# An attention and mixture-of-experts layer on one core: normalised input recomputed from kept moments, output bias by a product with ones, routing by maximum and minimum, counts by one scan

## The chip, the cores and the metric

The kernel runs on one core of a Trainium2 chip, written in Bass with semaphores placed by hand. The metric is the device time of one launch in microseconds (us). The engines are named as the profile names them: PE (TensorE; PEld is its weight load), DVE (VectorE), ACT (ScalarE), POOL (GpSimd), SP (SyncE, whose queue SPq issues nearly all DMAs).

## The reference, cut to what matters

```python
xn = _layernorm(x)                          # x: (2, 2048, 256) float32, no weights
x = x + _L0_attn_ref(xn, ...) + _L0_ffn_ref(xn, ...)

# inside _L0_ffn_ref(hidden_states = xn, ...), T = 4096 tokens, E = 16, D = 256, F = 1024
resid = hidden_states
x = layer_norm(hidden_states, ln1_w, ln1_b)
...                                          # q, k, v, causal attention, 16 heads of 16
hidden = resid + (ctx @ o_w + o_b)
resid = hidden
xt = layer_norm(hidden, ln2_w, ln2_b).reshape(T, D)
logits = xt @ router_w
probs = softmax(logits)
top1 = argmax(probs);  m1 = one_hot(top1, E)
top2 = argmax(where(m1 > 0, -inf, logits));  m2 = one_hot(top2, E)
loc1 = cumsum(m1, axis=0) - 1.0
loc2 = cumsum(m2, axis=0) - 1.0 + m1.sum(axis=0, keepdims=True)
m1 = m1 * (loc1 < C);  m2 = m2 * (loc2 < C)   # C = 512 places per expert
...                                          # gates, slots, 16 experts, combine
return resid + moe_out
```

Two attentions are computed, one with low-rank projections and one inside the feed-forward reference. Both read the normalised input `xn`, which is also the residual of the second part.

## The kernel before, in words

`layer` runs five stages one after the other, each an own block with a barrier between. Tokens are handled in 8 chunks of 512 (`NCH`, `CH`), a chunk being 4 tiles of 128 tokens (`TPC`).

**Stage A** (`stage_a`) loads x chunk by chunk, normalises it (`first_norm`, into `xn`), normalises that again for the second attention (`second_norm`, into `hn`), and makes q, k and v of both attentions in 17 PSUM units per chunk. q and k are split in two parts each (ACT writes the high part, DVE the low one) and stored in DRAM. SP issues, per chunk: the store of `xn` to the scratch tensor `xn_dram` (line 138), the load of x for the chunk after next (line 140), 16 stores of q and k parts (line 149), 2 stores of v (line 154). After chunk 5 it also issues the 14 loads of the first attention group (`load_piece`, lines 69 and 74). They stand in one queue.

**Stage B** (`stage_b`) is the two attentions, 16 groups of heads in an order written out by hand. The change leaves it as it is.

**Stage C** (`stage_c`) makes `hidden`, the second layer norm `xt` and the router's logits. For chunk c, PE computes `front(c)`: two PSUM banks of ctx @ o_w, 8 matmuls, which the trace records as 16 instructions. POOL computes `bias(c)`: o_b added in place to the chunk of `xn` loaded from DRAM (line 824). DVE computes `moments(c)`: bank + biased `xn` into `hidden` (line 862), then the statistics. ACT takes the root (line 901). DVE computes `norm(c)`: subtract and scale (line 882), times ln2_w (885), plus ln2_b (886), giving `xt_now`. PE then computes `back(c)`: 8 transposes (948), a wait for ACT's copies of them, and the logits (951). POOL also adds x to `hidden` into `base` (837), and once multiplies the last attention group by its reciprocals (841), behind the chunk 1 sum. Each engine has its own order: PE does front(0), front(1), and then for each c front(c+2) and back(c); DVE does moments(0), and then for each c moments(c+1) and norm(c); ACT root(c+1), back(c). Three places hold the loaded chunks, and SP loads chunk c+3 once the sum of chunk c is done.

**Stage D** (`stage_d`) routes. DVE works through one chain: softmax of the logits, `choose(0)`, `choose(1)`, `find_slots(0)`, `find_slots(1)`, the gates, and 8 rounds of `spread_tokens`, each of which builds one-hot matrices of 8 tiles. Nearly every step waits for the one ahead (`settle`). PE's order is fixed: 4 units of the output projection (`unit`, lines 1032 and 1034), `counts(0)`, 2 units, `counts(1)`, 10 units, and only then `collect`, which multiplies the one-hot matrices. `counts(n)` (lines 1040, 1041) sums the masks of choice n over the partitions and is what `find_slots(n)` waits for. `spread_tokens` has 4 places for its results (`RING`), so round 4 waits until `collect` has used round 0.

**Stage E** (`stage_e`) runs the 16 experts.

Of the kernel before, what the change touches and what calls it, by code (L numbers as in the profile page):

```python
# [76 lines left out]
def stage_a(nc, x, scratch, const, keep):  # L77

    xn_dram, q_dram, k_dram, v_dram = scratch
# [8 lines left out]
    with ExitStack() as ctx:  # L88
# [30 lines left out]
        xn_stored = [sem(f"xn_stored{i}") for i in range(2)]  # L119
# [5 lines left out]
        xn_chunks = xn_dram.rearrange("(c j p) d -> c p j d", j=TPC, p=P)  # L125
# [6 lines left out]
        def _(sp):  # L132
            for n in range(2):
                sp.dma_start(xs[:, n], x_chunks[n]).then_inc(x_in[n], 16)
            for c in range(NCH):
                u, b, cc = c % 2, c // (NCH // B), c % (NCH // B)
                sp.wait_ge(xn_ready, c + 1)
                sp.dma_start(xn_chunks[c], xn[:, u]).then_inc(xn_stored[u], 16)
# [22 lines left out]
            for n in range(2):  # L161
                sp.wait_ge(xn_stored[n], 16 * (NCH // 2))
                sp.wait_ge(v_stored[n], 16 * NCH)
# [4 lines left out]
        def _(dve):  # L168
# [5 lines left out]
            def norm(c, n, src, dst):  # L174
# [12 lines left out]
                dve.wait_ge(norm_step, done + 2)  # L187
                for j in range(TPC):
# [4 lines left out]
            def first_norm(i, u):  # L193
# [4 lines left out]
                dve.wait_ge(xn_stored[par], i * 16 + 16 * (u // 2))  # L198
                norm(c, 0, xs[:, par], xn[:, par]).then_inc(xn_ready, 1)
# [533 lines left out]
def stage_c(nc, x, scratch, const, keep):  # L733

    xn_dram, ctx_dram, xt_dram, rec_dram = scratch
# [4 lines left out]
    with ExitStack() as ctx:  # L740
# [7 lines left out]
        xn = sb("c_xn", [P, PLACES, TPC, D])  # L748
# [16 lines left out]
        biased = sem("biased")  # L765
# [17 lines left out]
        xn_chunks = xn_dram.rearrange("(c j p) d -> c p j d", j=TPC, p=P)  # L783
        xt_chunks = xt_dram.rearrange("(c j p) d -> c p j d", j=TPC, p=P)
        ARRIVED = 16 * 3

        @block.sync
        def _(sp):
            def load(c):
# [3 lines left out]
                sp.dma_start(xn[:, n], xn_chunks[c]).then_inc(arrived[n], 16)  # L793
# [27 lines left out]
        def _(pool):  # L821
            def bias(c):
                pool.wait_ge(arrived[c % PLACES], ARRIVED * (c // PLACES + 1))
# [5 lines left out]
            bias(0)  # L829
            for c in range(NCH):  # L830
                if c + 1 < NCH:
                    bias(c + 1)
# [11 lines left out]
        def _(dve):  # L844
# [8 lines left out]
            def moments(c):  # L853

                u = c % 2
                dve.wait_ge(biased, c + 1)
# [45 lines left out]

# [698 lines left out]
```

## Time and profile before

| what | value |
|---|---|
| median of 3 runs | 2394.43 us (2391.33 to 2430.84) |
| profiled execution | 2401.85 us, of which the span of the trace is 2400.1 us |
| mean granted PE clock | 0.95 of full speed |
| PE busy | 2243.1 us, 93% of the span |
| DVE busy | 1901.0 us, 79% |
| ACT busy | 1513.8 us, 63% |
| POOL busy | 495.8 us, 21% |

The shares are averages over five stages. Stage B alone takes from 227.9 to 1819.5 us, so that a share of the whole says little of the stages around it, which is where the change lies. Stages A, C and D have to be read in their own stretches of the trace. The 1.75 us by which the profiled execution is longer than its span lie outside the trace.

### The profile page before, as it was taken

The numbers are of one execution on the slowest core, as the hardware profiler recorded it, in microseconds if no ns is written. First come the engines' busy times: TensorE is split into PE (matmuls) and PEld (weight loads), VectorE is DVE, ScalarE is ACT, GpSimd is POOL, SyncE is SP. The second block draws the span as 40 slices with busy tenths as digits, with TensorE's granted clock in tenths as the row PEclk, the third lists the DMA queues.
The fourth block names the chain that finished last, engine by engine and source line by source line (L and its number), as shares of the span: only waits on it lengthen the run. The fifth ranks groups of instructions, "written<-read, shape, count | busy, mean of one in ns | idle before, by whom it ended". The sixth has DMA issues, their size and how long they took to land. (4 is left out here: it accounts for less than half of the span.)

```text
span 2400.1 us, 45293 instructions
## 1 busy us (share of the span) xinstructions
PE 2243.1 (93%) x15977; PEld 1289.1 (54%) x15977; DVE 1901.0 (79%) x5771; ACT 1513.8 (63%) x3190; POOL 495.8 (21%) x405
## 2 busy tenths in 40 slices
PE   5995999999999999999999999999996796999997
PEld 2553444444444444444444444444434675999997
DVE  3552999989999999898898998998944796666664
ACT  2541388778788787787777877877782212545443
POOL 0001000120211201202001011010004304777765
PEclk9997699999999999999999998999997798999999
DMA  5998325254154352441524516335115454445541
GB/s 154 292 267 226 36 29 64 36 66 57 27 73 51 41 64 39 63 57 27 73 36 57 64 23 78 42 42 69 16 20 155 148 172 115 109 111 120 125 118 31
DMA packets 145060, 203.62 MB, mean 85 GB/s; under 512 B 61066, under 2 KB 107872, under 8 KB 136544
## 3 DMA queue, kind: packets, MB, share of 16 engines
q1 hardware_dynamic: 132576, 191.08, 40.6%
q0 software_dynamic: 12288, 10.05, 3.3%
q8 instruction: 108, 1.77, 0.3%
q14 instruction: 88, 0.72, 0.1%
HBM read 134.24 MB, written 71.83 MB: 86 GB/s over the span
## 5 line engine op out<-in xcount | busy, mean ns | idle before, releaser
L652 ACT ACTIVATE probs<-s_banks 128x512 f32<-128x512 f32 (+3 forms) x2560 | 1182.4, 538 | 326.3 <-PE s_banks L603 198.3
L689 DVE TENSOR_REDUCE rowmax<-m_banks 128x1 f32<-128x512 f32 x1536 | 966.2, 682 | 66.8 <-PE m_banks L614 61.4
L614 PE MATMUL m_banks<-ks,qs 48*128 48x512 f32 (+3 forms) x2560 | 827.5, 436 | 28.6 <-PEq L88 20.5
L603 PE MATMUL s_banks<-qs,ks 50*128 50x512 f32 (+3 forms) x2560 | 819.7, 429 | 15.3 <-ACT probs L652 8.1
L632 PE MATMUL v_bank<-probs,vs 128*32 128x512 f32 (+3 forms) x5120 | 619.2, 556 | 0.0
L603 PEld LDWEIGHTS s_banks<-qs,ks 50*128 50x128 f32 x2560 | 401.5, 188 | 397.6 <-ACT probs L652 359.9
L614 PEld LDWEIGHTS m_banks<-ks,qs 48*128 48x128 f32 x2560 | 415.5, 193 | 262.0 <-DVE rowmax L689 162.9
L686 DVE CUSTOM_DVE_ANT_0 unused<-m_banks,c_maskq 128x128 bf16<-128x128 f32 (+3 forms) x1024 | 466.8, 486 | 59.9 <-issue 51.8
L549 POOL CAST nparts<-negmax 128x16 fp32r<-128x16 f32 x64 | 12.6, 197 | 1190.1 <-DVE negmax L695 1190.1
L1436 PE MATMUL e_banks<-w_parts,hid_parts 128*128 128x256 f32 x1536 | 189.7, 284 | 2.2 <-DVE hid_parts L1355 2.2
L575 PE MATMUL s_banks<-c_identb,c_later_col 64*128 64x64 bf16 x1024 | 188.8, 196 | 0.0
L575 PE MATMUL s_banks<-c_identb,c_later_col_swapped 64*128 64x64 bf16 x1024 | 188.5, 196 | 0.0
L1436 PEld LDWEIGHTS e_banks<-w_parts,hid_parts 128*128 128x128 f32 x1536 | 185.6, 192 | 3.8 <-DVE hid_parts L1355 2.5
L632 PEld LDWEIGHTS v_bank<-probs,vs 128*32 128x32 f32 x5120 | 101.5, 108 | 157.5 <-issue 80.4
L1421 PE MATMUL e_banks<-xinT,w_parts 128*128 128x512 f32 x768 | 179.4, 393 | 1.5 <-DVE xinT L1340 1.5
L1389 ACT ACTIVATE hid_parts<-e_banks,c_b1T 128x512 fp32r<-128x512 f32 x128 | 89.7, 701 | 114.7 <-PE e_banks L1421 102.8
L1421 PEld LDWEIGHTS e_banks<-xinT,w_parts 128*128 128x128 f32 x768 | 144.7, 190 | 31.5 <-issue 1.9
L1355 DVE TENSOR_TENSOR hid_parts<-e_hid,hid_parts 128x512 fp32r<-128x512 f32 x128 | 97.3, 776 | 47.3 <-ACT e_hid L1390 47.3
L1308 POOL DMA_INDIRECT out<-scaled,sums_of x64 | 113.1, 1767 | 36.9 <-POOL scaled L1302 23.3
L575 PEld LDWEIGHTS s_banks<-c_identb,c_later_col 64*128 64x128 bf16 x1024 | 95.4, 96 | 26.7 <-issue 6.2
L575 PEld LDWEIGHTS s_banks<-c_identb,c_later_col_swapped 64*128 64x128 bf16 x1024 | 94.8, 96 | 24.3 <-issue 12.1
L1302 POOL TENSOR_SCALAR scaled<-eout,slot_gates 128x256 f32<-128x256 f32 x64 | 95.9, 1545 | 54.5 <-DVE eout L1365 54.5
(185 smaller groups left out, 1744.1 us busy)
## 6 DMA issues: line engine op xcount, KB each, us to landing
w<-in_L_ffn_fc_w SPq DMA_DIRECT2D x32, 1024.0 KB, 4.9
qs<-q_scratch SPq DMA_DIRECT2D x96, 256.0 KB, 8.3
ks<-k_scratch SPq DMA_DIRECT2D x96, 256.0 KB, 10.0
q_scratch<-parts SPq DMA_DIRECT2D x64, 256.0 KB, 4.4
k_scratch<-parts SPq DMA_DIRECT2D x64, 256.0 KB, 4.5
v_scratch<-vt SPq DMA_DIRECT2D x16, 512.0 KB, 7.7
v_in<-v_scratch SPq DMA_DIRECT2D x32, 256.0 KB, 10.9
qs<-mrows SPq DMA_DIRECT2D x512, 2.0 KB
```

What stands on the lines that cost most here:

```text
L575: ins = pe.matmul(bank[:, j * HALF:(j + 1) * HALF], const[mask][rows, :], const["identb"][rows, rows], start=False, stop=j == 1)
L603: ins = pe.matmul(bank, ks[rows, slot, h // 2, k * P:(k + 1) * P], qs[rows, slot, h // 2, q * CH + first:(q + 1) * CH], start=True, stop=n ...
L614: pe.matmul(room(("M", NM * group + n))[:, 0:width], qs[rows, slot, h // 2, t * P:(t + 1) * P], ks[rows, slot, h // 2, c * CH:c * CH + wid ...
L632: ins = pe.matmul(v_bank[rows, first:CH], vs[:, slot, k, rows], probs[:, (n * GH + h) % PR, 0:CH - first], start=k == 0, stop=k == TPC * ( ...
L652: act.activation(probs[:, n % PR, 0:width], s_banks[:, (NS * group + n) % SRING, 0:width], ACT.Exp, scale=SCALE).then_inc(p_ready, 1)
L686: dve.tensor_tensor_reduce(unused[:, h, 0:width], scores, const["maskq"][:, CH - width:CH], 1.0, NEG, ALU.add, ALU.max, out).then_inc(m_us ...
L689: dve.tensor_reduce(out, scores, AX.X, ALU.max).then_inc(m_used, 1)
L1302: pool.tensor_scalar(scaled[:, u, j, :], eout[:, u, j, :], slot_gates[:, TPE * e + j:TPE * e + j + 1], None, ALU.mult).then_inc(weighed, 1)
L1308: pool.indirect_dma_start(out=rows, out_offset=bass.IndirectOffsetOnAxis(ap=sums_of[:, TPE * e + j:TPE * e + j + 1], axis=0), in_=scaled[: ...
L1355: dve.tensor_tensor(hid_parts[:, LO, f, :], hid[:, f % HRING, :], f32(hid_parts[:, HI, f, :]), ALU.subtract).then_inc(hid_split, 1)
L1421: last = pe.matmul(banks[:, HBANK + f % HRING, :], w1_parts[:, a, h, f * P:(f + 1) * P], xinT[:, b, h, :], start=h == 0 and (a, b) == PASS ...
L1436: last = pe.matmul(banks[:, OBANK + n, j * D:(j + 1) * D], hid_parts[:, a, f, tile * P:(tile + 1) * P], w2_parts[:, b, f, :], start=f == 0 ...
```

## The change

In stage A, `first_norm` keeps the reciprocal deviation and the negated mean of every token (`first_rstd`, `first_minus`, two small DVE instructions per chunk), and `xn` is no longer stored. In stage C nothing loads it. ACT makes `centred` = x - mean (`centre(c)`, 4 instructions per chunk), DVE multiplies by the kept reciprocal and adds the PSUM bank in one instruction per tile, and o_b enters the bank by one more matmul per tile: a row of ones times the row of o_b. POOL's bias step is gone. In stage D the two choices are found by a maximum, a comparison and a minimum over the expert's numbers, the totals are counted in expert order, and one scan over 512 columns with a zero at each expert's start replaces 16 scans over 32; several pairs of DVE instructions are joined to one.

```diff
@@ stage_a
-                sp.dma_start(xn_chunks[c], xn[:, u]).then_inc(xn_stored[u], 16)
...
+                if tiles is not None:
+                    dve.tensor_copy(const["first_rstd"][:, tiles], rstd[:, :])
+                    dve.tensor_scalar(const["first_minus"][:, tiles], meanvar[:, :, 0], -1.0, None, ALU.mult)
@@ stage_c, SP
-        ARRIVED = 16 * 3
+        ARRIVED = 16 * 2
-                sp.dma_start(xn[:, n], xn_chunks[c]).then_inc(arrived[n], 16)
@@ stage_c, POOL
-                pool.tensor_tensor(xn[:, c % PLACES], xn[:, c % PLACES],
-                                   const["ob"][:, :].unsqueeze(1).to_broadcast([P, TPC, D]), ALU.add).then_inc(biased, 1)
@@ stage_c, DVE
                 for half in range(2):
-                    pair = slice(2 * half, 2 * half + 2)
                     dve.wait_ge(front_ready, c * FRONT + half + 1)
-                    dve.tensor_tensor(hidden[:, u, pair, :], banks[:, BACK + u * FRONT + half, :].rearrange("p (j d) -> p j d", d=D),
-                                      xn[:, c % PLACES, pair, :], ALU.add).then_inc(hidden_ready, 1)
+                    for j in range(2):
+                        tile = 2 * half + j
+                        last = dve.scalar_tensor_tensor(out=hidden[:, u, tile, :], in0=centred[:, c % PLACES, tile, :],
+                                                        scalar=const["first_rstd"][:, c * TPC + tile:c * TPC + tile + 1],
+                                                        in1=banks[:, BACK + u * FRONT + half, j * D:(j + 1) * D],
+                                                        op0=ALU.mult, op1=ALU.add)
+                    last.then_inc(hidden_ready, 1)
@@ stage_c, ACT
+            def centre(c):
+                act.wait_ge(arrived[c % PLACES], ARRIVED * (c // PLACES + 1))
+                for j in range(TPC):
+                    last = act.activation(centred[:, c % PLACES, j, :], xs[:, c % PLACES, j, :], ACT.Identity,
+                                          bias=const["first_minus"][:, c * TPC + j:c * TPC + j + 1])
+                last.then_inc(centred_ready, 1)
+            centre(0)
+            centre(1)
             root(0)
             for c in range(NCH):
                 if c + 1 < NCH:
                     root(c + 1)
+                if c + 2 < NCH:
+                    centre(c + 2)
                 back(c)
@@ stage_c, PE, front(c)
                         for h in range(KD):
                             last = pe.matmul(bank[:, j * D:(j + 1) * D], attT[:, c % PLACES, h, tile * P:(tile + 1) * P],
-                                             const["ow"][:, h, :], start=h == 0, stop=h == KD - 1)
+                                             const["ow"][:, h, :], start=h == 0, stop=False)
+                        last = pe.matmul(bank[:, j * D:(j + 1) * D], const["ones"][0:1, :], const["ob"][0:1, :], start=False, stop=True)
@@ stage_d, PE, counts(n)
-                pe.matmul(banks[:, COUNTS + 2 * n + 1, :], const["ones"][:, :], m, start=True, stop=True).then_inc(counted, 1)
+                by_expert = mask[n][:, :, :].rearrange("p t e -> p e t")
+                pe.matmul(banks[:, COUNTS + 2 * n + 1, :], const["ones"][:, :], by_expert, start=True, stop=True).then_inc(counted, 1)
@@ stage_d, DVE, choose(n)
-                for t in range(NTILE):
-                    ins = dve.max(top8[:, t, :], src[:, t, :])
-                settle(ins)
-                for t in range(NTILE):
-                    ins = dve.max_index(top8_id[:, t, :], top8[:, t, :], src[:, t, :])
-                settle(ins)
-                settle(dve.tensor_copy(expert[n][:, :], top8_id[:, :, 0]))
-                dve.tensor_tensor(mask[n][:, :, :], experts.rearrange("p (t e) -> p t e", e=E), wide(expert[n][:, :]),
-                                  ALU.is_equal).then_inc(masks_ready, 1)
+                settle(dve.tensor_reduce(one[:, :], src[:, :, :], AX.X, ALU.max))
+                settle(dve.tensor_tensor(work[:, :, :], src[:, :, :], wide(one[:, :]), ALU.is_equal))
+                settle(dve.scalar_tensor_tensor(out=work[:, :, :].rearrange("p t e -> p (t e)"),
+                                                in0=work[:, :, :].rearrange("p t e -> p (t e)"), scalar=-float(E), in1=experts,
+                                                op0=ALU.mult, op1=ALU.add))
+                settle(dve.tensor_reduce(expert[n][:, :], work[:, :, :], AX.X, ALU.min))
+                dve.tensor_tensor(mask[n][:, :, :], work[:, :, :], wide(expert[n][:, :]), ALU.is_equal).then_inc(masks_ready, 1)
@@ stage_d, DVE, find_slots(n)
-                settle(dve.tensor_copy(total[:, :, :], banks[:, COUNTS + 2 * n + 1, :].rearrange("p (t e) -> p t e", e=E)))
-                for e in range(E):
-                    ins = dve.tensor_tensor_scan(upto[n][:, :, e], ones_cube[:, :], total[:, :, e], 0.0, ALU.mult, ALU.add)
-                settle(ins)
+                by_expert = banks[:, COUNTS + 2 * n + 1, :]
+                settle(dve.tensor_tensor_scan(upto[n][:, :], same_expert[:, :], by_expert, 0.0,
+                                              ALU.mult, ALU.add))
...
-                settle(dve.tensor_scalar(place[:, :, :], place[:, :, :], -1.0, None, ALU.add))
...
-                settle(dve.tensor_scalar(work[:, :, :], place[:, :, :], float(CAP), None, ALU.is_lt))
-                settle(dve.tensor_tensor(kept[n][:, :, :], work[:, :, :], mask[n][:, :, :], ALU.mult))
+                settle(dve.scalar_tensor_tensor(out=kept[n][:, :, :].rearrange("p t e -> p (t e)"),
+                                                in0=place[:, :, :].rearrange("p t e -> p (t e)"), scalar=float(CAP),
+                                                in1=mask[n][:, :, :].rearrange("p t e -> p (t e)"), op0=ALU.is_lt, op1=ALU.mult))
```

The part left out in `find_slots` joins the subtraction of one to the sum of places, and of the 11 instructions on 32 columns behind the slots makes 7.

On PE in stage C, this is what stands for front(2) and back(0) before; `c_ow` is o_w, `attT` the loaded context, `c_rw` the router's weights.

```order
L932 MATMUL c_banks<-c_ow,attT 128x256 [waits hidden_ready,arrived2]
L932 MATMUL c_banks<-c_ow,attT 128x256 x3
L932 MATMUL c_banks<-c_ow,attT 128x256 [waits hidden_ready]
L932 MATMUL c_banks<-c_ow,attT 128x256 x3
L948 MATMUL c_banks<-c_ident,xt_now 128x128 [waits c_xt_ready]
L948 MATMUL c_banks<-c_ident,xt_now 128x128 x7
```

And this is the same place in the changed kernel.

```order
L935 MATMUL c_banks<-c_ow,attT 128x256 [waits hidden_ready,arrived2]
L935 MATMUL c_banks<-c_ow,attT 128x256
L937 MATMUL c_banks<-c_ob,c_ones 128x256
L935 MATMUL c_banks<-c_ow,attT 128x256 x2
L937 MATMUL c_banks<-c_ob,c_ones 128x256
L935 MATMUL c_banks<-c_ow,attT 128x256 [waits hidden_ready]
L935 MATMUL c_banks<-c_ow,attT 128x256
L937 MATMUL c_banks<-c_ob,c_ones 128x256
L935 MATMUL c_banks<-c_ow,attT 128x256 x2
L937 MATMUL c_banks<-c_ob,c_ones 128x256
L952 MATMUL c_banks<-c_ident,xt_now 128x128 [waits c_xt_ready]
```

Four matmuls of 256 columns stand in front(c) that were not there; nothing else of PE's order moves.

On ACT in stage C the start before is this.

```order
L901 ACT_TABLE_LOAD
L901 ACTIVATE c_std<-c_meanvar,c_eps 128x4 [waits c_var_ready] x2
L912 ACTIVATE xtT<-c_banks 128x512 [waits back_ready] x2
L912 ACTIVATE logits<-c_banks 128x64 [waits back_ready]
L901 ACTIVATE c_std<-c_meanvar,c_eps 128x4 [waits c_var_ready]
```

In the changed kernel it is this.

```order
L898 ACTIVATE centred<-c_xs,c_first_minus 128x256 [waits arrived0]
L898 ACTIVATE centred<-c_xs,c_first_minus 128x256 x3
L898 ACTIVATE centred<-c_xs,c_first_minus 128x256 [waits arrived1]
L898 ACTIVATE centred<-c_xs,c_first_minus 128x256 x3
L893 ACT_TABLE_LOAD
L893 ACTIVATE c_std<-c_meanvar,c_eps 128x4 [waits c_var_ready] x2
L898 ACTIVATE centred<-c_xs,c_first_minus 128x256 [waits arrived2]
L898 ACTIVATE centred<-c_xs,c_first_minus 128x256 x3
L911 ACTIVATE xtT<-c_banks 128x512 [waits back_ready] x2
```

The table load moved behind two chunks of `centred`, and a wait for chunk c+2's loads now stands ahead of back(c)'s copies.

## Rows read from the trace of the kernel before

**Rows 1.** Busy time by stretch: us, PE, PEld, DVE, ACT, POOL, PEclk, DMA share, GB/s
```profile
1819.50:1918.00 98.50, 69.61 (x320) 59.39 (x320) 70.03 (x145) 13.79 (x33) 46.95 (x23) 0.74 0.61 182
...
147.00:168.00 21.00, 19.03 (x68) 11.34 (x67) 11.09 (x36) 10.73 (x19) 0.00 (x0) 1.00 0.96 301
205.00:210.00 5.00, 2.55 (x12) 1.90 (x10) 2.48 (x4) 1.87 (x4) 0.00 (x0) 1.00 1.04 388
```

**Rows 2.** Timeline of SP in stage A: start, us, instruction, times
```profile
181.82 11.34 SPq L138 DMA_DIRECT2D xn_scratch<-xn  x1
...
205.75 1.20 SPq L138 DMA_DIRECT2D xn_scratch<-xn  x1
```

**Rows 3.** Timeline of PE in stage C, in brackets the idle time ahead
```profile
1826.93 13.89 PE L932 MATMUL c_banks<-c_ow,attT 128*128 128x256 f32 x48 [8.31 <-DMA c_xs<-in_L_attn_x]
1850.16 1.97 PE L948 MATMUL c_banks<-c_ident,xt_now 128*128 128x128 f32 x8 [9.34 <-DVE xt_now L886]
...
1856.25 5.62 PE L932 MATMUL c_banks<-c_ow,attT 128*128 128x256 f32 x16
1861.71 1.04 PE L948 MATMUL c_banks<-c_ident,xt_now 128*128 128x128 f32 x8
...
1865.29 3.70 PE L932 MATMUL c_banks<-c_ow,attT 128*128 128x256 f32 x16
...
1891.67 6.67 PE L932 MATMUL c_banks<-c_ow,attT 128*128 128x256 f32 x16
```

**Rows 4.** Timeline of DVE in stage C
```profile
1839.69 3.72 DVE L882 TENSOR_SCALAR xt_now<-hidden,c_meanvar,c_rstd 128x256 f32<-128x256 f32 x4
...
1844.70 5.40 DVE L886 TENSOR_TENSOR xt_now<-xt_now,c_ln2b 128x1024 f32<-128x1024 f32 x1
...
1861.91 0.69 DVE L862 TENSOR_TENSOR hidden<-c_banks,c_xn 128x512 f32<-128x512 f32 x1 [1.07 <-PE c_banks L932]
...
1864.56 1.60 DVE L882 TENSOR_SCALAR xt_now<-hidden,c_meanvar,c_rstd 128x256 f32<-128x256 f32 x4
...
1868.59 1.28 DVE L862 TENSOR_TENSOR hidden<-c_banks,c_xn 128x512 f32<-128x512 f32 x2
...
1879.99 5.08 DVE L882 TENSOR_SCALAR xt_now<-hidden,c_meanvar,c_rstd 128x256 f32<-128x256 f32 x4
```

**Rows 5.** Timeline of POOL in stage C
```profile
1843.45 5.57 POOL L841 TENSOR_TENSOR rden<-rden,pv_last 128x2048 f32<-128x2048 f32 x1 [0.84 <-DMA rden<-rec_scratch]
...
1879.57 2.35 POOL L824 TENSOR_TENSOR c_xn<-c_xn,c_ob 128x1024 f32<-128x1024 f32 x1 [6.38 <-DMA c_xs<-in_L_attn_x]
```

**Rows 6.** Timeline of DVE in stage D
```profile
1922.06 2.54 DVE L1132 MAX8 top<-d_probs 128x8 f32<-128x16 f32 x32
...
1939.32 0.69 DVE L1149 COPY d_total<-d_banks 128x512 f32<-128x512 f32 x1
1940.05 2.09 DVE L1151 TENSOR_TENSOR_SCAN upto<-ones_cube,d_total 128x32 f32<-128x32 f32 x16
...
1947.43 0.18 DVE L1165 TENSOR_SCALAR d_one<-slot 128x32 f32<-128x32 f32 x1
...
1949.85 0.69 DVE L1149 COPY d_total<-d_banks 128x512 f32<-128x512 f32 x1
...
1954.61 2.72 DVE L1159 TENSOR_TENSOR d_place<-d_place,upto 128x512 f32<-128x512 f32 x1
...
1969.36 0.69 DVE L1181 TENSOR_TENSOR in_cell<-numbers,cell 128x512 f32<-128x512 f32 x1
...
1996.11 0.22 DVE L1205 TENSOR_SCALAR d_row<-d_banks 128x64 f32<-128x64 f32 x1 [2.14 <-PE d_banks L1047]
```

**Rows 7.** Timeline of PE in stage D
```profile
1936.81 1.02 PE L1041 MATMUL d_banks<-mask,c_ones 128*128 128x512 f32 x2
...
1943.71 1.02 PE L1041 MATMUL d_banks<-mask,c_ones 128*128 128x512 f32 x2
...
1970.03 0.59 PE L1034 MATMUL d_banks<-base,c_ident 128*128 128x256 f32 x2
```

More of the change, by code:

```diff
@@ L77, in stage_a @@
 def stage_a(nc, x, scratch, const, keep):
-    xn_dram, q_dram, k_dram, v_dram = scratch
+    q_dram, k_dram, v_dram = scratch
     UNITS = 17
@@ L172, in _, with norm @@
             dve.memset(none[:, 3:4], 0.0).then_inc(unit_ready, 2 * UNITS)
-            def norm(c, n, src, dst):
+            def norm(c, n, src, dst, tiles=None):
                 done = c * 4 + 2 * n
@@ L197, in first_norm @@
                 dve.wait_ge(unit_ready, c * UNITS + C_UNIT)
-                dve.wait_ge(xn_stored[par], i * 16 + 16 * (u // 2))
-                norm(c, 0, xs[:, par], xn[:, par]).then_inc(xn_ready, 1)
+                norm(c, 0, xs[:, par], xn[:, par], bass.ds(i * (2 * TPC) + u * TPC, TPC)).then_inc(xn_ready, 1)
             def second_norm(i, u):
@@ L855, in moments @@
                 u = c % 2
[L856 removed]
+                dve.wait_ge(centred_ready, c + 1)
                 if c >= 2:
@@ L986, in stage_d @@
         kept = [sb(f"kept{n}", cube) for n in range(2)]
-        upto = [sb(f"upto{n}", cube) for n in range(2)]
-        place, total, work = sb("d_place", cube), sb("d_total", cube), sb("d_work", cube)
-        top8 = sb("top8", [P, NTILE, 8])
-        top8_id = sb("top8_id", [P, NTILE, 8], U32)
+        upto = [sb(f"upto{n}", [P, E * NTILE]) for n in range(2)]
+        place, work = sb("d_place", cube), sb("d_work", cube)
         expert = [sb(f"expert{n}", flat) for n in range(2)]
@@ L1148, in find_slots @@
                 dve.wait_ge(counted, n + 1)
-                settle(dve.tensor_copy(total[:, :, :], banks[:, COUNTS + 2 * n + 1, :].rearrange("p (t e) -> p t e", e=E)))
-                for e in range(E):
-                    ins = dve.tensor_tensor_scan(upto[n][:, :, e], ones_cube[:, :], total[:, :, e], 0.0, ALU.mult, ALU.add)
-                settle(ins)
-                settle(dve.tensor_tensor(work[:, :, :], upto[n][:, :, :], total[:, :, :], ALU.subtract))
-                settle(dve.tensor_tensor(place[:, :, :], banks[:, COUNTS + 2 * n, :].rearrange("p (t e) -> p t e", e=E),
-                                         work[:, :, :], ALU.add))
@@ L1157, in find_slots @@
+                settle(dve.scalar_tensor_tensor(out=place[:, :, :].rearrange("p t e -> p (t e)"), in0=banks[:, COUNTS + 2 * n, :],
+                                                scalar=-1.0, in1=work[:, :, :].rearrange("p t e -> p (t e)"),
+                                                op0=ALU.add, op1=ALU.add))
                 if n == 1:
-                    firsts = upto[0][:, NTILE - 1:NTILE, :].to_broadcast(cube)
+                    firsts = upto[0][:, :].rearrange("p (e t) -> p t e", e=E)[:, NTILE - 1:NTILE, :].to_broadcast(cube)
@@ L1166, in find_slots @@
                 for q in range(2, TPE):
-                    settle(dve.tensor_scalar(two[:, :], slot[n][:, :], float(q * P), None, ALU.is_ge))
-                    settle(dve.tensor_tensor(one[:, :], one[:, :], two[:, :], ALU.add))
-                settle(dve.tensor_scalar(two[:, :], one[:, :], -float(P), None, ALU.mult))
-                settle(dve.tensor_tensor(slot[n][:, :], slot[n][:, :], two[:, :], ALU.add))
-                settle(dve.tensor_scalar(two[:, :], any_kept[n][:, :], -float(CELLS), float(CELLS), ALU.mult, ALU.add))
-                settle(dve.tensor_tensor(one[:, :], one[:, :], two[:, :], ALU.add))
-                settle(dve.tensor_scalar(two[:, :], expert[n][:, :], float(TPE), None, ALU.mult))
+                    settle(dve.scalar_tensor_tensor(out=one[:, :], in0=slot[n][:, :], scalar=float(q * P), in1=one[:, :],
+                                                    op0=ALU.is_ge, op1=ALU.add))
+                settle(dve.scalar_tensor_tensor(out=slot[n][:, :], in0=one[:, :], scalar=-float(P), in1=slot[n][:, :],
+                                                op0=ALU.mult, op1=ALU.add))
+                settle(dve.scalar_tensor_tensor(out=one[:, :], in0=expert[n][:, :], scalar=float(TPE), in1=one[:, :],
+                                                op0=ALU.mult, op1=ALU.add))
+                settle(dve.tensor_scalar(two[:, :], any_kept[n][:, :], -float(CELLS), float(CELLS + E * TPE), ALU.mult, ALU.add))
                 settle(dve.tensor_tensor(cell[n][:, :], one[:, :], two[:, :], ALU.add))
@@ L1543, in layer @@
                   "ln1w": [P, KD], "ln1b": [P, KD], "qb": [P, KD], "kb": [P, KD], "ln2w": [P, D], "ln2b": [P, D],
-                  "b1T": [P, E * F // P], "ident": [P, P], "upper": [P, P], "ones": [P, P], "eps": [P, 1], "maskq": [P, CH]}
+                  "b1T": [P, E * F // P], "ident": [P, P], "upper": [P, P], "ones": [P, P], "eps": [P, 1], "first_rstd": [P, NTILE], "first_minus": [P, NTILE], "maskq": [P, CH]}
         const = {n: ctx.enter_context(nc.sbuf_tensor(f"c_{n}", s, F32)) for n, s in shapes.items()}
@@ L1572, in layer @@
                     nc.sbuf_tensor("numbers", [P, NUMBERS_SIZE], F32) as numbers:
-                stage_c(nc, x, (xn_dram, ctx_dram, xt_dram, rec_dram), const, ((base, logits, numbers), last))
+                stage_c(nc, x, (ctx_dram, xt_dram, rec_dram), const, ((base, logits, numbers), last))
                 stage_d(nc, (w["fc1_w"], w["fc2_w"]), (ctx_dram, xt_dram, out), const, (base, logits, numbers), keep)
```

25 lines of the change are left out of this document (9 added, 16 removed).

## The prediction

> **What bounds the kernel now.** I read the busy times by stretch first, then the timelines of the stretches that the change touches. The reader is to see that each has another bound, so that no share of the whole span prices an edit.
>
> Stage A: in a chunk's 21 us PE is busy 19.0 at full clock while the DMA engines are busy 0.96 [rows 1]. PE paces it and the DMA is just behind. Once the loads for the attention are queued as well, SP stands 11.34 us in the issue of one store of `xn` [rows 2], and at 205 to 210 us the DMA share is over 1 at 388 GB/s while PE is half idle [rows 1]. So the end of stage A is paced by DMA.
>
> Stage C: 98.5 us, PE busy 69.6, DVE 70.0, the granted clock 0.74 on the mean [rows 1]. Neither fills it. PE's undisturbed turn is a back of 1865.29 - 1861.71 = 3.58 us and a front of 3.70, less 0.16 by which instructions overlap: 7.1 us [rows 3]. DVE's is longer, because some of its instructions last several times their size: four of line 882 take 1.60 us at one place, 3.72 and 5.08 at others, and one of line 886 takes 5.40 us [rows 4]. At those places POOL runs: its multiply from 1843.45 for 5.57 us, its bias from 1879.57 [rows 5]. DVE waits for POOL there. These instructions read only SBUF. The Trainium skill ("SBUF — State Buffer", section "SBUF: two separate sides") says that DVE instructions with two SBUF inputs or in a two-port mode and GpSimd lock one port pair for a whole instruction; the rows agree.
>
> Stage D: DVE's chain runs from 1922.06 to 1996.11 [rows 6]; PE's units end at 1970.03 + 0.59 = 1970.6 [rows 7], and only behind them can the one-hot products start. DVE's first round starts at 1969.36 [rows 6], so the two arrive together. That decides the worth of a shorter routing.
>
> **Stage A, part by part.** Eight stores of 0.52 MB go. Six of them lie where PE paces: nothing is gained. Two, at 181.82 and 205.75 [rows 2], lie in the stretch that DMA paces: at 388 GB/s 1.35 us each, 2.7 us. The second blocked SP for 1.20 us, which agrees. If only the second counts it is 1.35; at the 301 GB/s of the paced chunk [rows 1] and with a third store's backlog carried in, 5.2. I keep 1 to 6 as ends. I take -3.0, near the saturated row. The 11.34 us of the first is a wait for room in the queue; the next store inherits it. Two instructions of 4 columns are added on DVE before each `xn`; beyond the first chunk DVE is half idle, and in the first they cost some 0.2 us.
>
> **Stage C, start.** The first chunk's loads shrink from three of 0.52 MB to two. They landed at 1826.93, 7.4 us behind the stage's start [rows 3]; a third of what is beyond 2 us of latency is 1.6 us, so PE starts at about 1825.3. But each front now has 24 instructions for 16. At full clock one is 3.70 / 16, less the overlap of the last, 0.216 us; at the lower level, half the clock, 0.43. The first bank needs 12 instructions for 8 while PE is at the lower level (1.7 us more), which eats the gain: hidden(0) is ready at the same time as now. Front(1) is 1.7 us longer, so moments(1) ends at 1841.6 instead of 1839.5. Norm(0) then meets POOL's long multiply, as now: its loads come earlier, but the sum of chunk 1 stands ahead of it on POOL and ends 1842.3, the multiply at 1847. DVE finishes norm(0) at about 1850.6; now 1844.70 + 5.40 = 1850.1 [rows 4]. So +0.5 there. ACT's `centre` is hidden: four instructions of 256 columns in the 8 us in which ACT waits, its table load too, and PE's product is later than both. The new wait for chunk c+2's loads ahead of back(c)'s copies is covered: those loads are issued two turns before.
>
> **Stage C, middle.** PE, idle since 1844, does back(0) at the lower level as now (6.1 us [rows 3]). Front(3) took 5.62 us, its clock rising at its end; with 24 instructions it ends at about 1864.0 instead of 1861.9, and hidden(3) comes 2.1 us later than now. From there PE's turn is 24 x 0.216 = 5.2 for the front and 3.58 for the back, 8.8 us. DVE's turn, freed of the bias: 1868.59 - 1864.56 = 4.03 for norm, 1864.56 - 1861.91 = 2.65 for half of hidden and the statistics, 0.6 for its other half (1.28 for both) [rows 4], and 0.1 to 0.3 because hidden is four instructions for two at the same columns (four of line 882 take 1.60, two of line 862 1.28): about 7.5. **PE takes over as the bound**, and what DVE is freed of is late nowhere. Four such turns behind front(3): 1864.0 + 4 x 8.8 = 1899.2 for front(7)'s end, where it now ends at 1891.67 + 6.67 = 1898.3 [rows 3], because DVE's turns and the clock hold it there. The tail, DVE's norm(6) and (7) and two backs, is the same. So stage C loses 0.8 us if PE stays at its full clock. But front(7) now runs mostly at the lower level, 3.0 us longer (6.67 for 3.70 [rows 3]); PE has smaller gaps in the change, so I take three quarters of one such front, 2.3. Stage C: **+3.1 us**. The nearest rows bound a K=1 matmul by the price of the full one above and by nothing below; at zero stage C would fall to DVE's turn, -6 to -7 us. The price by columns is the nearer: the records of equal columns are equal in the trace, whatever the tile. The Trainium skill ("TensorE: Matmul & The Clock Gate", section "Why this matters for your kernels") says that a single matmul with 32 rows takes as long as one with 128. No row here has a matmul of one row; by that page the sum stays as it is.
>
> **Stage D.** A choice is now (1939.32 - 1922.06 - 3 x 0.73) / 2 = 7.5 us without mask and second logits, an instruction of 512 columns being 0.73 with its wait (1940.05 - 1939.32 [rows 6]). The new one has four: 2.9. Both masks are ready at 1922.06 + 5 x 0.73 + 0.73 + 5 x 0.73 = 1930.0 instead of 1939.3. **But find_slots(0) waits for counts(0)**, whose place on PE is behind four units: it ends at 1936.81 + 1.02 = 1937.8 [rows 7]. Of 9.3 us saved 1.5 arrive. Find_slots(0) took 10.5 us (1949.85 - 1939.32). Now: a scan, six of 512 columns at 0.73, seven small at 0.22 (11 took 1949.85 - 1947.43). The scan over 512 columns lies between 0.69, a copy of as many, and 2.1, the sixteen; from 2.09 / 16 = 0.130 for 32 columns, at 1 column per cycle or 2 cycles per column, I take 1.15. Sum 7.1: to 1944.9. Counts(1) ends at 1944.7, just in time. Find_slots(1) has one more of 512: 7.8, to 1952.7. The gates took 4.2, and POOL's split of w1 (which held line 1159 for 2.72 instead of 0.69 and the next one too, 4.1 us) comes at the same time by ACT's clock and is met again, now by the gates: 1961.0. Four rounds of 3.07 ((1993.97 - 1969.36) / 8, the last ending 2.14 before 1996.11): 1973.3. Round 4 needs the first `collect`, behind the units: 1970.6 + 1.9 = 1972.5. So the rounds go on without a wait: last at 1985.5, its product 2.1 later, 1987.6 for 1996.11. **-8.5 us**; -9.3 is the most while PE's units stand, -8 with a slower scan, -6.5 if the strided reads of the counts double them. The Trainium skill ("DVE: opcode table, instruction layouts, handler registers and perf-mode slots", section 6) says that this scan runs at half throughput, which would be an estimated 1.13 us; the trace's 32-column scans fit it, and the sum would not move.
>
> **Sum.** -3.0 + 0.2 + 3.1 - 8.5 = -8.2 us on a span of 2400.1. The profiled execution, 2401.85, would be 2393.6; that execution lies 7.4 above the median, and the prediction is put on the median: 2394.4 - 8.2 = **2386 us**. A gain or loss of some 2% (48 us) is about what a measurement of this kernel can tell from no change.
>
> **Rivals.** (1) DVE still paces stage C, because a product with ones is cheap: DVE's 7.5 us turn for four chunks is 30.0 where the ends of front(3) and front(7) now lie 1898.3 - 1861.9 = 36.4 apart [rows 3]: -6.4 instead of +3.1, total -17.7, 2377. For it: only one row of the array is filled. Against: records go by columns. 0.17. (2) Slower: PE sits at its lower clock through stage C. There the mean is 0.74 already, and the idle time ahead of back(0) stays (6 to 7 us). At the lower level a turn of 8.8 is 16.5. Two more of the five turns that way (+15.4) give +7, 2402; all five +30, 2425. It decides against the change from about one turn on (8.2 / 7.7). 0.13. (3) The stage A relief is larger, since the DMA share of 0.96 is nearly a bound in each chunk: every store worth 1.35, 11 us: 2378. Against: PE is dense there. 0.06. (4) The routing is not held by PE's order and the whole 16 us arrive: 2378. Against: the orders are fixed in program. 0.04. My forecast: 0.60.
>
> **How the numbers follow.** The forecast's own bounds are -1 to -6 in A, -2 to +8 in C, -9.3 to -6.5 in D: 2377 to 2396. Rivals 1, 3 and 4 stretch the low end to 2374, rival 2 the high end to 2400, beyond which part of it stays. No case but the extreme of rival 2 nears 48 us: faster 0.01, within 0.97, slower 0.02.
>
> **What the profile would show.** Right: the time from stage C's start to its end 98 to 105 us, PE's front rows at x24 and about 5.3 us with no wait of line 882 over 2 us except by the multiply; DVE in stage D idle about 7 us ahead of the scan, released by the count's matmul; the one-hot rounds without gaps; stage A shorter by 3. Wrong: a front of 24 in under 4.5 us, PE's clock under 0.6 in stage C, DVE's wait ahead of the scan missing, or stage B or E changed by several us, which nothing here prices.

## The result and the profile after

The changed kernel took 2456.39 us (median of 4, 2447.35 to 2475.16) beside 2398.84 us for the kernel before: ratio 1.0228, 95% interval 1.0182 to 1.0275. It is slower, by 44 to 66 us, where 2386 was forecast; whether by more than 2% the interval leaves open. The profiled execution took 2475.16 us, its span 2473.4.

By stretch the place is plain. These are windows of the changed kernel: stage B, stage C, and the 81 us from stage D's start; the columns are those of [rows 1].

```profile
223.20:1841.60 1618.40, 1594.14 (x12352) 739.14 (x12352) 1413.23 (x4689) 1215.65 (x2689) 159.92 (x169) 0.94 0.37 46
...
1842.40:1999.27 156.87, 144.31 (x384) 93.51 (x384) 65.54 (x161) 27.30 (x65) 25.50 (x15) 0.51 0.30 88
1999.27:2080.27 81.00, 64.45 (x329) 54.61 (x330) 58.93 (x98) 13.36 (x20) 9.39 (x6) 0.90 0.46 137
```

Stage C lasts 156.9 us for 98.5 [rows 1], 58.4 more. DVE does less there than before (65.5 us for 70.0), PE is busy 144.3 us for 69.6, and its granted clock fell from 0.74 to 0.51 (of its two levels the lower is 0.50). Stage B takes 1618 us for 1592, which the change doesn't touch; in the twelve kernels below, which share stage B, it took 1588 to 1619 with no relation to the edit. That is scatter of single executions, not the change (the other three of this kernel had spans of 2445.6 to 2458.3).

PE's timeline in stage C shows why it is busy:

```profile
1848.08 2.07 PE L935 MATMUL c_banks<-c_ow,attT 128*128 128x256 f32 x4 [6.61 <-DMA c_xs<-in_L_attn_x]
...
1904.60 1.97 PE L952 MATMUL c_banks<-c_ident,xt_now 128*128 128x128 f32 x8
1907.26 3.59 PE L955 MATMUL c_banks<-c_rw,xtT 128*128 128x16 f32 x16 [0.69 <-ACT xtT L911]
1910.69 2.05 PE L935 MATMUL c_banks<-c_ow,attT 128*128 128x256 f32 x4
1912.67 1.22 PE L937 MATMUL c_banks<-c_ob,c_ones 1*128 1x256 f32 x2
1913.82 2.08 PE L935 MATMUL c_banks<-c_ow,attT 128*128 128x256 f32 x4
...
1923.28 1.97 PE L952 MATMUL c_banks<-c_ident,xt_now 128*128 128x128 f32 x8
```

PE waits for little more than ACT's copies, 0.69 us a turn (a turn is the time from one chunk's back to the next one's), and yet every instruction has its price at the lower level: eight transposes are 1.97 us, where they were 1.04 in an undisturbed turn [rows 3]. The turn is 1923.28 - 1904.60 = 18.68 us; all eight chunks go that way. From 1848.08 to the first back at 1885.92 PE runs three fronts without a wait, and the level doesn't change. Before, the same three took 13.89 us [rows 3], less than 48 x 0.43 = 20.6, so the clock came up within them. A tile takes 1913.82 - 1910.69 = 3.13 us, though six instructions of 256 columns at 0.43 are 2.6. The rest is seen in the weight loads:

```profile
1848.08 1.35 PEld L935 LDWEIGHTS c_banks<-c_ow,attT 128*128 128x128 f32 x4 [6.88 <-DMA c_xs<-in_L_attn_x]
1850.09 0.50 PEld L937 LDWEIGHTS c_banks<-c_ob,c_ones 1*128 1x128 f32 x2 [0.65 <-issue]
1851.23 1.35 PEld L935 LDWEIGHTS c_banks<-c_ow,attT 128*128 128x128 f32 x4 [0.65 <-issue]
```

At each change between 128 rows and one, the load stands still for 0.65 us before it starts: it isn't drawn ahead of the running matmul, as it is between instructions of equal rows. A tile has two such switches, and its 0.55 us beyond the columns make some 0.3 us of each. The 32 tiles of the stage have some 18 us of them, which the trace counts as busy time of PE. DVE now waits for PE at each half:

```profile
1898.50 0.87 DVE L851 SCALAR_TENSOR_TENSOR hidden<-centred,c_first_rstd,c_banks 128x256 f32<-128x256 f32 x2 [5.52 <-PE c_banks L937]
1904.71 0.87 DVE L851 SCALAR_TENSOR_TENSOR hidden<-centred,c_first_rstd,c_banks 128x256 f32<-128x256 f32 x2 [5.34 <-PE c_banks L937]
```

In stage D the DVE's chain came shorter as meant. Its rows, and PE's of the count ahead of it:

```profile
2019.88 1.22 DVE L1152 TENSOR_TENSOR_SCAN upto<-same_expert,d_banks 128x512 f32<-128x512 f32 x1 [8.03 <-PE d_banks L1044]
2021.13 1.03 DVE L1154 TENSOR_TENSOR d_work<-upto,d_banks 128x512 f32<-128x512 f32 x1
...
2027.98 1.22 DVE L1152 TENSOR_TENSOR_SCAN upto<-same_expert,d_banks 128x512 f32<-128x512 f32 x1 [0.64 <-PE d_banks L1044]
...
2070.15 0.23 DVE L1208 TENSOR_SCALAR d_row<-d_banks 128x64 f32<-128x64 f32 x1 [2.14 <-PE d_banks L1050]
```

```profile
2017.03 1.02 PE L1042 MATMUL d_banks<-mask,c_upper 128*128 128x512 f32 x2
2017.89 1.88 PE L1044 MATMUL d_banks<-mask,c_ones 128*128 128x512 f32 x2
```

From the stage's start to the last product's reading it is 2070.15 - 1999.27 = 70.9 us for 1996.11 - 1918.0 = 78.1 [rows 1, 6]: 7.2 less.

### The profile page after: what moved, and what is told of

The parts are those of the page before. It is cut to its first block and busy times, and to the rows that moved or that the text cites. A ratio compares the mean times of both kernels' runs of the same rounds, so it can differ in the third digit from the quotient of the medians.

```text
span 2473.4 us, 45239 instructions
## 1 busy us (share of the span) xinstructions
PE 2341.5 (95%) x16041; PEld 1325.7 (54%) x16041; DVE 1883.0 (76%) x5574; ACT 1526.5 (62%) x3222; POOL 473.1 (19%) x397
## 5 line engine op out<-in xcount | busy, mean ns | idle before, releaser
L630 PE MATMUL v_bank<-probs,vs 128*32 128x512 f32 (+3 forms) x5120 | 635.8, 570 | 0.0
```

The costliest lines, as they stand in the source:

```text
L630: ins = pe.matmul(v_bank[rows, first:CH], vs[:, slot, k, rows], probs[:, (n * GH + h) % PR, 0:CH - first], start=k == 0, stop=k == TPC * ( ...
```

## The experiments

The theory (A): a product with few rows takes PE's clock away in all of stage C, and nothing else in the change costs. The rivals: (B) any six instructions for four overload PE, whatever their rows; (C) the loss is in the recomputation (ACT's centring, the new waits, the loads). All runs stand in one table, then one by one. Stage C is counted from its first load's issue to stage D's, in one profiled execution. Where the last column says "one run", that execution is all there is, and no ratio is given. Two kernels leave something out of the result: "no product" all of o_b, "in one tile of four" o_b in three tiles of four.

| kernel | stage C, us | clock in it | ratio to before (95%) |
|---|---|---|---|
| before | 98.5 | 0.74 | |
| changed: 1 row | 156.9 | 0.51 | 1.0228 (1.0182 to 1.0275) |
| before with the 1-row product alone | 158.6 | 0.51 | 1.0221 (1.0148 to 1.0294) |
| 32 rows | 156.9 | 0.51 | 1.0193 (1.0113 to 1.0272) |
| 64 rows | 156.8 | 0.51 | one run |
| 96 rows | 107.3 | 0.75 | one run |
| 128 rows | 103.9 | 0.78 | 0.9997 (0.9954 to 1.0040) |
| 128 rows, 127 of them zero | 102.9 | 0.77 | 0.9996 (0.9955 to 1.0037) |
| 1 row, in one tile of four | 105.6 | 0.71 | one run |
| 1 row, two products together | 125.1 | 0.69 | one run |
| no product, no o_b | 83.5 | 0.80 | 0.9880 (0.9803 to 0.9958) |
| o_b by POOL again | 94.8 | 0.77 | 0.9981 (0.9939 to 1.0024) |
| 128 rows of bf16 | 91.9 | 0.77 | 0.9918 (0.9890 to 0.9946) |
| before with stage D's part alone | 101.5 | 0.75 | 0.9976 (0.9953 to 0.9998) |

**The product alone, put into the kernel before.**

```diff
@@ kernel before, stage_c: bias(c) of POOL removed, DVE waits for the loads
-                                             const["ow"][:, h, :], start=h == 0, stop=h == KD - 1)
+                                             const["ow"][:, h, :], start=h == 0, stop=False)
+                        last = pe.matmul(bank[:, j * D:(j + 1) * D], const["ones"][0:1, :], const["ob"][0:1, :], start=False, stop=True)
```

> The kernel before with only one part of the change: o_b by the one-row product, POOL's bias step gone, everything else as before; nothing is left out. Theory A: this part alone gives the whole loss: PE at its lower clock through stage C, turn 18 to 19 us, stage C about 158 us, the time 1.02 to 1.03 of before. Theory C: stage C no slower than 105 us.

It has the whole loss: 158.6 us, 1.0221. Theory C falls, since nothing is recomputed here.

**No product.** The product with ones is removed from the changed kernel.

> The changed kernel without the product with ones: o_b is left out of the result. Theory A and theory B both: PE's front is 16 instructions again and the clock as before, stage C paced by DVE at about 7.6 us a turn, 88 to 98 us in all, the time 0.987 to 0.995 of before. A third theory (C: ACT's centring or the shorter loads slow stage C): stage C stays over 120 us.

83.5 us. DVE's turn, freed of POOL's bias, is the pace: the rows of line 874 lie 1879.82 - 1872.18 = 7.64 apart.

```profile
1872.18 1.60 DVE L874 TENSOR_SCALAR xt_now<-hidden,c_meanvar,c_rstd 128x256 f32<-128x256 f32 x4
...
1879.82 1.59 DVE L874 TENSOR_SCALAR xt_now<-hidden,c_meanvar,c_rstd 128x256 f32<-128x256 f32 x4
```

**128 rows of ones** (o_b divided by 128, made once by DVE; `ob_part`).

```diff
-                        last = pe.matmul(bank[:, j * D:(j + 1) * D], const["ones"][0:1, :], const["ob"][0:1, :], start=False, stop=True)
+                        last = pe.matmul(bank[:, j * D:(j + 1) * D], const["ones"][0:128, :], ob_part[0:128, :], start=False, stop=True)
```

> The changed kernel with o_b brought in by a product of 128 rows of ones with 128 equal rows of o_b / 128, in place of one row of each; nothing is left out. Theory A (products with one row keep PE at its lower clock and make their neighbours' weight loads wait): PE reaches full clock in stage C, the turn falls from 18.7 to about 9 us, stage C from 158 to about 102 us, the time to 0.99 to 1.00 of before. Theory B (any extra product in the front does it, because the fronts and backs together are what keeps the clock low): stage C stays over 140 us and the time at 1.02 of before.

The count, the columns and the result are the same, and stage C is 53 us shorter. Theory B falls as the cause of the loss. By the rows above, some 18 us of the 53 are the switches, and the other 35 are the clock (an estimate from 32 tiles at 0.55 us). What B has right is smaller: the product of 128 rows still costs 103.9 us for 83.5 without one. PE's rows, all at full clock but for the front's start at 1879.81:

```profile
1876.09 1.04 PE L955 MATMUL c_banks<-c_ident,xt_now 128*128 128x128 f32 x8
...
1879.81 2.05 PE L938 MATMUL c_banks<-c_ow,attT 128*128 128x256 f32 x4
...
1886.61 1.04 PE L955 MATMUL c_banks<-c_ident,xt_now 128*128 128x128 f32 x8
1888.39 1.96 PE L958 MATMUL c_banks<-c_rw,xtT 128*128 128x16 f32 x16 [0.74 <-ACT xtT L914]
1890.19 1.11 PE L938 MATMUL c_banks<-c_ow,attT 128*128 128x256 f32 x4
1891.14 0.59 PE L940 MATMUL c_banks<-ob_part,c_ones 128*128 128x256 f32 x2
...
1895.46 1.04 PE L955 MATMUL c_banks<-c_ident,xt_now 128*128 128x128 f32 x8
```

The turn from 1886.61 is 8.85 us, a tile 0.95 + 0.43, without a switch's gap. The backs ahead of it start at 1855.02, 1865.56 and 1876.09, so the three turns before took 10.5 us each, with the first instructions of each front at the lower level: the clock falls for some microseconds in these even with full rows.

**32, 64 and 96 rows**, the same edit with another number.

> As the run with 128 rows, but 32 rows of ones times 32 rows of o_b / 32. Theory A, if what counts is the share of the rows filled: between one row and 128, PE at full clock for part of stage C, 105 to 140 us. If what counts is that the product spans fewer rows than the next one at all: as with one row, 150 us or more. Theory B: as with one row.

> The changed kernel with 64 rows in the product (ones times o_b / 64). One and 32 rows gave the same stage C of 157 to 158 us, 128 rows 104. If the loss grows as rows are left empty, 64 rows lie between, near 130 us. If it has an edge between 32 and 128 rows, 64 give one of the two, 104 or 157. If it comes from changing the rows between two instructions (the weight load is then not hidden), 64 rows give 157.

> The changed kernel with 96 rows in the product (ones times o_b / 96). One, 32 and 64 rows gave 157 us for stage C, all with the clock at 0.51; 128 rows 103 to 104. If only a full array counts, or if the switch between row counts does it, 96 rows give 157 too; if there is an edge in the number of rows below 96, they give 104.

32 and 64 rows are as slow as one, 96 nearly as fast as 128. There is an edge between 64 and 96. The first product of the stage, 64 rows and then 96:

```profile
1818.77 1.22 PE L940 MATMUL c_banks<-ob_part,c_ones 64*128 64x256 f32 x2
```

```profile
1826.84 1.06 PE L940 MATMUL c_banks<-ob_part,c_ones 96*128 96x256 f32 x2
```

Both are at the lower level, and the 64 rows last 0.16 longer; 128 rows take 1.06 there too. The weight loads of 96 rows have no idle time ahead of them at either level (the row shown is at full clock), those of 64 have 0.65 us as with one row:

```profile
1830.32 0.41 PEld L940 LDWEIGHTS c_banks<-ob_part,c_ones 96*128 96x128 f32 x2
```

```profile
1818.77 0.50 PEld L940 LDWEIGHTS c_banks<-ob_part,c_ones 64*128 64x128 f32 x2 [0.65 <-issue]
```

So the edge in the clock and the edge in the switch lie in the same interval of rows.

**Rows or data.** 128 rows are named, of which 127 hold zero.

```diff
+            settle(dve.memset(first_row[:, :], 0.0))
+            dve.memset(first_row[0:1, :], 1.0).then_inc(ob_ready, 1)
-                        last = pe.matmul(bank[:, j * D:(j + 1) * D], const["ones"][0:1, :], const["ob"][0:1, :], start=False, stop=True)
+                        last = pe.matmul(bank[:, j * D:(j + 1) * D], first_row[:, :], const["ob"][:, :], start=False, stop=True)
```

> The changed kernel with a left side of 128 rows in the product, of which only the first is not zero, and o_b's 128 equal rows as the right side: the sum is exactly o_b, as in the changed kernel, and only the rows that the instruction spans differ. If what counts is the rows that the instruction names, stage C comes out as with 128 rows of ones, 104 us and a ratio of 1.00. If what counts is data that are not zero, or only the work done, it comes out as with one row: a turn of 18.7 us, stage C 155 to 160 us, ratio 1.02.

Stage C took 102.9 us. The rows that the instruction names count, not what is in them.

**How many, and how divided.** First one product for four tiles (`if tile == 0`), then as many as in the changed kernel, two at a time:

```diff
+                for j in range(2):
+                    for k in range(FRONT):
+                        pe.matmul(fronts[k][:, j * D:(j + 1) * D], const["ones"][0:1, :], const["ob"][0:1, :], start=True, stop=False)
+                    for k in range(FRONT):
+                        tile = 2 * k + j
+                        for h in range(KD):
...
```

> The changed kernel with the one-row product in the first tile of each chunk alone; o_b is left out of the other three tiles. If each product costs what it lasts, a quarter of the loss against the kernel without products is left: (158 - 83.5) / 4, stage C 102 us. If a few such products are enough to hold the clock down, PE stays at 0.5 and a turn is 18.7 less three products of 0.61 and three switches of 0.3: 16.0 us, stage C 135 us. If it takes many to hold it down, the clock is up again in most of the stage and stage C is under 95 us.

> The changed kernel with the same one-row products, as many and as long, but two of them together (one for each bank) ahead of the tiles that they belong to, so that PE changes between 128 rows and one four times in a chunk instead of eight, and runs eight instructions of 128 rows in a row instead of four. If it is the share of time in products of few rows that holds the clock down, it stays at 0.51 and a turn is 18.7 less two pairs of switches, 4 x 0.3 = 1.2 at most: 17.5 us, stage C 147 to 152 us. If it is the switch, or how long PE runs full arrays without a break, the clock comes up in part or in whole: stage C 105 to 130 us. One product in four tiles, with sixteen in a row between, gave 105.6 with the clock up in the first chunk.

One in four gave 105.6 us, near what the first case of its expectation said (102), but not for its reason: the clock came up while one-row products went on, and sank again. The pairs gave 125.1, below what the share of time says (147 to 152). The clock changes inside the stage, at the same instructions. These are the rows of the pairs:

```profile
1845.21 2.07 PE L933 MATMUL c_banks<-c_ob,c_ones 1*128 1x256 f32 x4
1847.21 3.78 PE L937 MATMUL c_banks<-c_ow,attT 128*128 128x256 f32 x8
1850.92 1.13 PE L933 MATMUL c_banks<-c_ob,c_ones 1*128 1x256 f32 x4
1851.98 2.00 PE L937 MATMUL c_banks<-c_ow,attT 128*128 128x256 f32 x8
...
1903.77 2.07 PE L933 MATMUL c_banks<-c_ob,c_ones 1*128 1x256 f32 x4
```

So the share of time in few rows alone doesn't decide: as many of them, in fewer and longer pieces, let the clock up now and then, to 0.69 on the mean. At full clock the weight loads still wait at each change of rows, 0.33 us for 0.65.

**o_b by POOL, xn made by ACT** (scale and bias in one pass, the kept constant being the mean times the reciprocal deviation).

> The changed kernel without the product: stage A keeps the mean times the reciprocal deviation, ACT makes the whole normalised input in stage C, and POOL adds o_b to it as in the kernel before; stages A and D as changed. Stage A is 4.7 us shorter than before and stage D 7.0; stage C keeps the turns of the kernel before with its first loads 1.7 us earlier: 95 to 100 us. Sum -12 to -15 us, ratio 0.994 to 0.995. If the changed kernel's loss were in the recomputation and not in the product, stage C would stay at 150 us and the ratio over 1.015.

Stage C is 94.8, just under the expected 95 to 100; the ratio is 0.9981, with an interval that takes in both one and the expected 0.994. So the recomputation doesn't cause the loss. POOL's step costs here too: line 860 waits 2.25 us for it in two of the last four chunks.

**128 rows of bf16.** o_b as three bf16 parts in rows 0, 32 and 64, the others zero.

```diff
+            for i in range(3):
+                last = dve.tensor_copy(ob_rows[32 * i:32 * i + 1, :], ob_b[i][32 * i:32 * i + 1, :])
...
-                        last = pe.matmul(bank[:, j * D:(j + 1) * D], const["ones"][0:1, :], const["ob"][0:1, :], start=False, stop=True)
+                        last = pe.matmul(bank[:, j * D:(j + 1) * D], ones_b[:, :], ob_rows[:, :], start=False, stop=True)
```

> The changed kernel with o_b in three bf16 parts (their sum is o_b to 24 bits) in rows 0, 32 and 64 of a 128-row right side that is zero elsewhere, and a 128-row left side of bf16 ones. A float32 product of 256 columns is two instructions; in bf16 it is one. If what counts is the rows that an instruction spans, and the rest is plain columns, PE stays at full clock and a front costs 3.70 + 4 x 0.11 = 4.1 us, PE's turn 7.6 like DVE's 7.64: stage C 84 to 87 us, ratio 0.987 to 0.992, faster than both kernels. If bf16 or rows of zeros keep the clock down, stage C is at 130 or over. If the change of type costs a switch, at most 0.3 us twice a tile, a turn is 9 to 10 us and stage C 95 to 105 us.

It took 2385.36 us beside 2403.61: **0.9918, faster than the kernel before** by 0.5 to 1.1%, and by its ratio faster than the changed one. A product is one instruction, and the next matmul starts 0.11 us behind it (1838.59 - 1838.48):

```profile
1838.48 0.27 PE L952 MATMUL c_banks<-ob_rows,ones_b 128*128 128x256 bf16 x1
1838.59 1.03 PE L950 MATMUL c_banks<-c_ow,attT 128*128 128x256 f32 x4
...
1883.40 1.04 PE L967 MATMUL c_banks<-c_ident,xt_now 128*128 128x128 f32 x8
...
1890.97 1.04 PE L967 MATMUL c_banks<-c_ident,xt_now 128*128 128x128 f32 x8
```

PE's turn is 7.57 here and DVE's 7.64, so that neither waits for the other. Stage C was 91.9, not 84 to 87: POOL's multiply held line 882 for 5.40 us, and three of PE's turns took 11.8, 9.2 and 9.2, with part of each front at the lower level. One of them is the turn from the last row shown: the clock, once up, fell again.

**Stage D's part alone.**

> The kernel before with stage D of the changed kernel and nothing else. If stage D's gain is its own, DVE's chain there is 70.2 us for 78.0 and the time 7 to 8 us less: ratio 0.997. If the gain came from what stage C leaves (PE's clock, or loads issued at another time), the chain is 78 us as before. Stage C 98 to 99 us in both.

DVE's chain took 1990.70 - 1920.33 = 70.4 us for 78.1: the gain is its own. The 101.5 us of its stage C, whose code is that of before, show that one profile tells a stage to some 3 us.

```profile
1990.70 0.23 DVE L1204 TENSOR_SCALAR d_row<-d_banks 128x64 f32<-128x64 f32 x1 [2.14 <-PE d_banks L1046]
```

## Why the prediction was wrong, point by point

**Stage A: agrees, within a wide scatter.** Stage B began at 223.3 for 228.1 in the first profiles, but the kernels without the store began it at 221.6 to 225.5 (mean 223.9 of 11), the three with it at 228.1, 228.0 and 224.3 (mean 226.8): -2.9 for the forecast -3.0. One of the three lies among the eleven, so that nearness to 3.0 is in part luck. The next store did inherit the wait for room:

```profile
179.63 13.93 SPq L146 DMA_DIRECT2D q_scratch<-parts  x4
```

**Stage C: wrong, +58.4 for +3.1.** The step that failed is "From there PE's turn is 24 x 0.216 = 5.2 for the front and 3.58 for the back, 8.8 us", with the sentence behind it that rests the price of the one-row matmul on its columns. For 128 rows the price is right: the one turn at full clock is 8.85. Three others took 10.5, since the clock fell in each, and that kernel's stage C was 103.9 us where the forecast says 101.6. With one row PE never reaches the full clock, so the price by columns held at a level that the product itself prevents, and the two switches of a tile, 0.55 us, stood nowhere in the sum. Rival 2 named the place, and the last part its mark ("PE's clock under 0.6 in stage C"), but with gaps as the cause, at 0.13 and at most +30. Its turn of 16.5 was 18.7 (the switches, four tiles of 0.6, were missing), and it was charged to five turns. In fact all eight fronts and backs are at the lower level: 8 x (12.6 + 6.1) = 150, with 5.7 ahead of the first. The reason given for few cold turns ("PE has smaller gaps in the change") is refuted: the gaps vanished and the clock fell. The gain at the stage's start was taken at 1.6 us; by its own working, a third of 7.4 - 2, it is 1.8, and PE did start 1.7 us earlier, 5.7 behind the stage's start for 7.4.

A hint stood in the trace of before. At stage B's start PE has only 48-row matmuls, is shown as busy nearly all the time and stays at the lower level (us, PE busy, clock, DMA share, GB/s):

```profile
238.00:248.00 10.00, 9.92 (x19) 0.50 0.00 0
248.00:258.00 10.00, 10.00 (x19) 0.50 0.00 0
```

It is no more than a hint, since PE does wait there. The records of its matmuls overlap, but each weight load stands 0.31 us until DVE's line 689 has read a bank, and the loads start 0.60 us apart:

```profile
238.30 0.28 PEld L614 LDWEIGHTS m_banks<-ks,qs 48*128 48x128 f32 x1 [0.31 <-DVE rowmax L689]
```

The Trainium skill's rule that a matmul with 32 rows lasts as long as one with 128 (page "TensorE: Matmul & The Clock Gate", section "Why this matters for your kernels") agrees where equal rows follow each other: four instructions of one row took 2.07 us in the pairs' run, four of 128 rows 2.04 to 2.05 in the run with 128 rows. Between full matmuls it holds less well: two instructions of one, 32 or 64 rows took 1.22 us at the lower level, two of 96 or 128 rows 1.06. The section doesn't say that the clock's level depends on the rows. The Trainium skill's section "Part 1: The HAM clock gate" in the same page has the clock follow how busy PE has been. In the profile's busy time this doesn't show: PE, busy 144.3 of 156.9 us, stayed at 0.51. With the 18 us of switches taken off it is still busy for 81% of the stage, where the kernel with 128 rows was busy 82.3 of 103.9 us, 79%, and had 0.78. What the chip itself counts as busy no run here shows.

**Rival 1** (DVE paces with a cheap product) had its mechanism right and its price too small: without the product stage C lost 15.0 us, not 6.4: DVE's turn was 7.64 us, as forecast (7.5). PE's earlier start, 1.7 us, and the mean clock, which rose from 0.74 to 0.80, go with it; the rival had counted neither, and no run parts them.

**Stage D: right, -7.2 for -8.5** (7.7 alone). The wait ahead of the scan is there, 8.03 us, released by the count. The scan was 1.22 for 1.15. The sum left out the strided reads, which the forecast had only as a case (-6.5): 1.03 to 1.05 us on DVE for 0.69 (three times), and PE's count read by expert, 1.88 us for 1.02, which delays the first scan by 0.86. The Trainium skill's half throughput for this scan ("DVE: opcode table, instruction layouts, handler registers and perf-mode slots", section 6) agrees: 1.22 us, where other instructions of 512 columns take 0.69.

**Rivals 3 and 4** did not come: -2.9, and 7.2 of 16. Of the whole, -2.9 + 58.4 - 7.2 = +48 lies in the measured 44 to 66.

**What stays open.** That naming fewer rows in the product brings the clock down is shown; how it does so is not. It can be the rows left empty, or PE standing some 0.3 us at each change of rows. Both have their edge between 64 and 96 rows, and the pairs changed both at once, with half as many changes. Two things speak for the rows. The busy shares above, 81% and 79%, are alike with the standing taken off. And in stage D of before, full-row matmuls kept a clock of 1.00 from 1980 to 1990 us, though PE waited 1.01 us in every 3.06. Neither is a test, since to hold a level is not to reach it. Against rows alone speaks that stage B later runs at 0.96 with matmuls of 48 and 50 rows among those of 128. No run has few-row matmuls with neither a wait nor a change of rows.

## What to carry to other kernels

A matmul's price by columns holds only at the clock that it leaves PE. Before a product of few rows is put between full ones, put it alone into the kernel and read PE's granted clock in that stage: here that one run (158.6 us at 0.51) has the whole loss. Name all 128 rows; zeros in them cost no more than ones (102.9 us beside 103.9). For a constant, use bf16 parts: the same bias takes 0.11 us per tile at full clock instead of 0.43, and the clock comes up as with float32 rows (0.77). A stage that is bound by two engines in turn is priced by the clock first, the instructions second.

## What was not expected of the hardware

- PE stayed at granted clock 0.51 for some 150 us with gaps of under 1 us in its records, with one, 32 or 64 rows in a third of the front's instructions; 0.75 to 0.78 with 96 or 128, zeros or not.
- A weight load is not drawn ahead across a change from 128 rows to 1, 32 or 64 or back (0.65 us idle and some 0.3 us per switch at the lower level, 0.33 us idle at full clock). Between 128 and 96 it is, and between float32 and bf16 of 128 rows.
- A matmul whose moving operand is read with a stride of 16 elements took 0.94 us for 0.51 (512 columns, two instructions 1.88 for 1.02); DVE's read with a stride of 32 elements 1.03 to 1.07 for 0.69.
